# Gated cross-attention and mixture-of-experts layer on one core: scores turned by plain transposes, joint first loads, key groups 3 and 4 in two parts, a last bank in two steps, and a new order of stages

## The reference, cut

```python
def xattn(text, features):                    # text: layernorm(x) per batch
    features_n = rmsnorm(features, fn_w)
    Q = rmsnorm(text @ Wq.T + Wq_b, qn_w)
    K = rmsnorm(features_n @ Wk.T + Wk_b, kn_w)
    scores = (Q @ K.T) / sqrt(1024)            # 512 x 64 per batch
    return softmax(scores) @ features_n
def ffn(x):
    base = x @ W_base.T + b_base
    gate = softmax(x @ W_gate.T); thr = sigmoid(x @ W_thr + b_thr) / 8
    w = relu(gate - thr); w = w / sum(w)       # 8 experts, rank 16
    return base + 2 * ((x @ A.T) * w) @ B
x = x + tanh(g_xattn) * xattn(layernorm(x), ctx)
x = x + tanh(g_ffn) * ffn(layernorm(x))
```

## Time and profile before

| what | value |
|---|---|
| median of 3 runs | 478.19 us |
| the profiled execution | 478.68 us |
| its span in the trace | 476.7 us |
| around the span | 1.98 us |
| PE busy | 471.1 us, 99% |
| DVE, ACT, POOL busy | 353.9, 172.4, 121.1 us |

### The profile page before, as it was taken

One profiled execution on the slowest core, in us unless ns is written; L12 is line 12 of the kernel. 1 busy time (PEld: TensorE's weight loads), 2 busy tenths in 40 slices (PEclk: granted clock), 3 DMA queues, 4 the chain that ended last, 5 costly groups with the idle time before them and its releaser, 6 DMA issues.

```text
span 476.7 us, 6939 instructions
## 1 busy us (share of the span) xinstructions
PE 471.1 (99%) x2482; PEld 401.3 (84%) x2482; DVE 353.9 (74%) x735; ACT 172.4 (36%) x347; POOL 121.1 (25%) x110
## 2 busy tenths in 40 slices
PE   8999999999999999999999999999999999999997
PEld 6888999998887888888898888888888887888885
DVE  1379896597888967869978888868677678877732
ACT  3795541341214304217326625332241521414300
POOL 1021511003353343345242406031220402305000
PEclk9999999999999999999999999999999999999999
DMA  8995219948676369466579640221405013050202
GB/s 267 411 411 197 84 58 409 382 167 294 196 240 242 134 237 289 187 244 237 183 267 420 280 141 35 78 100 46 133 0 178 0 63 114 1 177 1 89 1 88
DMA packets 22545, 84.39 MB, mean 177 GB/s; under 512 B 2672, under 2 KB 4720, under 8 KB 19696
## 3 DMA queue, kind: packets, MB, share of 16 engines
q1 hardware_dynamic: 22368, 83.94, 48.0%
q10 hardware_dynamic: 144, 0.02, 0.0%
HBM read 61.93 MB, written 22.02 MB: 176 GB/s over the span
## 4 chain that ended last, share of the span: by engine, by line
PE 91%; DMA 6%; DVE 1%; issue 1%; SPq 1%; POOL 0%; DVEq 0%
PE bank L637 11%; PE bank L758 11%; PE bank L762 10%; PE bank L760 10%; PE bank L673 6%; PE bank L675 6%; PE bank L674 6%; PE bank L736 4%; PE bank L516 3%; PE bank L601 2%; DMA out_dram<-xs 2%; DMA xz<-xt_dram 2%; PE bank L659 2%; PE bank L658 2%; PE bank L660 2%; PE bank L738 2%
## 5 line engine op out<-in xcount | busy, mean ns | idle before, releaser
L1532 POOL TENSOR_TENSOR small<-small,tiny 128x1 f32<-128x1 f32 (+2 forms) x25 | 22.7, 907 | 163.1 <-DVE small L1165 138.4
L1506 DVE SCALAR_TENSOR_TENSOR xs<-bank,tiny,xs 128x512 f32<-128x512 f32 x60 | 43.2, 748 | 21.0 <-PE bank L762 15.0
L673 PE MATMUL bank<-xth,gram 128*128 128x512 f32 x144 | 57.3, 398 | 0.0
L675 PE MATMUL bank<-xtl,gram 128*128 128x512 f32 x144 | 56.3, 391 | 0.0
L674 PE MATMUL bank<-xth,gram 128*128 128x512 f32 x144 | 56.1, 390 | 0.0
L1560 POOL TENSOR_TENSOR sq_sum<-sq_sum,sq 128x512 f32<-128x512 f32 x24 | 32.0, 1335 | 59.0 <-DVE sq L1340 59.0
L758 PE MATMUL bank<-wh_B,zh 128*128 128x512 f32 x116 | 47.0, 405 | 0.0
L758 PE MATMUL bank<-wh_T,zh 128*128 128x512 f32 x112 | 45.9, 410 | 0.0
L762 PE MATMUL bank<-wh_B,zl 128*128 128x512 f32 x116 | 45.6, 393 | 0.0
L760 PE MATMUL bank<-wl_B,zh 128*128 128x512 f32 x116 | 45.4, 391 | 0.0
L762 PE MATMUL bank<-wh_T,zl 128*128 128x512 f32 x112 | 44.1, 393 | 0.0
(11 more groups left out here) (200 smaller groups left out, 1117.8 us busy)
## 6 DMA issues: line engine op xcount, KB each, us to landing
xst<-x_dram SPq DMA_DIRECT2D x16, 512.0 KB, 4.3
xz<-xt_dram SPq DMA_DIRECT2D x16, 512.0 KB, 7.7
out_dram<-xs SPq DMA_DIRECT2D x14, 512.0 KB, 3.7
xa<-x_dram SPq DMA_DIRECT2D x12, 512.0 KB, 3.3
x<-xa SPq DMA_DIRECT2D x12, 512.0 KB, 2.8
xs<-x SPq DMA_DIRECT2D x12, 512.0 KB, 3.9
wq_raw<-wq_dram SPq DMA_DIRECT2D x8, 512.0 KB, 14.7
t_raw_T<-wb_dram SPq DMA_DIRECT2D x4, 1024.0 KB, 16.6
```

Of the source, the lines that this page charges most:

```text
L673: pe.matmul(acc[:, :], gram[:, g, 0, :], xth[b % 2][:, r, :], start=r == ROWS[j][0], stop=False)
L675: done = pe.matmul(acc[:, :], gram[:, g, 0, :], xtl[b % 2][:, r, :], start=False, stop=r == ROWS[j][-1])
L1506: dve.scalar_tensor_tensor(out=xs[slot][:, half(h)], in0=bank[C_BANK[n_bank]][:, :], scalar=tg[:, 1:2], in1=xs[slot][:, half(h)], op0=ALU. ...
```

## The change

Six edits. (1) Context and the first two key weights come in one array `front` and one load per chunk; the weights of group 2 are only issued once the first chunk has landed. (2) `RAW_KEYS` goes from 5 to 3: groups 3 and 4 use split operands; "ct_high" stands ahead of "k01", ("split", "CT", 0) behind group 2. The squares of the context move from ACT to DVE. (3) "tops": four transposes of `st_sb` (128 columns each) in place of the four matmuls with `ident2`; ACT copies one half out of the bank, DVE adds the other, and the maxima and exponentials read `pexp` in SBUF. (4) In the last pair "fin" 0 to 2 stand ahead of product P4, P4 and the last "fin" are made in two halves of 256 columns in two banks, and each half is evicted and stored alone, the second by ACT's queue. (5) `IDLE` 4 for 5. (6) The order of stages: ("x_stat", 0), "stat" 3, ("mr", 0), "rsb" with the first "k_out" and "load_hd" move.

```diff
-    RAW_KEYS = 5
+    RAW_KEYS = 3
...
-        IDLE = 5
+        IDLE = 4
...
+        def spans(p, n):
+            if (p, n) == (NP - 1, 3):
+                return [(C_BANK["D"], 0, HALF // 2), (H_BANKS[0], HALF // 2, HALF)]
+            return [(C_BANK[whole(p)[n][0]], 0, HALF)]
...
-                         ("gates", 0), ("split", "B12", 1), ("stat", 3)]
-                extra = {0: [("weights", 3), ("chosen", 0), ("hd", 0, 1), ("gates", 1), ("shares", 3), ("split", "B22", 0), ("fn_norm", 3),
+                         ("gates", 0), ("split", "B12", 1)]
+                extra = {0: [("weights", 3), ("chosen", 0), ("stat", 3), ("hd", 0, 1), ("gates", 1), ("shares", 3), ("split", "B22", 0), ("fn_norm", 3),
...
+                if (p, name) == (NP - 1, "P4"):
+                    last += [("fin", p, n) for n in range(3)]
                 last.append(("prod", p, i))
...
-                        if c % CK == 0:
-                            pe.wait_ge(ld_wk01[c // CK], 16)
                         pe.wait_ge((a_ct, v_ct)[c % 2], c // 2 + 1)
...
-                    acc = ring_open(("weights", b), "act")
+                    acc = ring_open(("weights", b), "dve")
                     pe.wait_ge(a_st, b + 1)
-                    for j in range(TPB):
-                        done = pe.matmul(acc[:, j * S:(j + 1) * S], st_sb[:, j * P:(j + 1) * P], ident2[:, :],
-                                         start=True, stop=True)
-                    done.then_inc(p_ring, 1)
+                    transposes(acc, st_sb[:, :].rearrange("p (j t) -> p j t", j=TPB))
...
-                load_ct(c)
-                sp.dma_start(wk01[:, :, kc, :], wk[0:2].rearrange("f p c m -> p f c m")[:, :, kc, :]).then_inc(ld_wk01[c], 16)
+                sp.dma_start(ct_wk01[:, :, c, :], front[:, c, :, :]).then_inc(ld_ct[c], 16)
+            sp.wait_ge(ld_ct[0], 16)
...
-                elif stage == "ctx_norm":
-                    for c in range(2):
-                        act.wait_ge(ld_ctx[c], 16)
-                        act.activation(ctx_sq[c][:, :], ctx_raw[c][:, :], ACT.Square,
-                                       accum_out=ctx_ss[:, c:c + 1]).then_inc(a_ctx, 1)
...
+                elif stage == "tops":
+                    b, = i
+                    n = ring.number["weights", b]
+                    act.wait_ge(p_ring, ring.full(("weights", b)))
                     if b > 0:
                         act.wait_ge(v_px, b)
...
+                    act.activation(pexp[:, :, :], bank[T_BANKS[n % 2]][:, :].rearrange("p (j h s) -> p j h s", j=TPB, h=2)[:, :, 0, :],
+                                   ACT.Copy).then_inc(a_top, 1)
...
+                    dve.wait_ge(a_top, b + 1)
+                    dve.tensor_tensor(pexp[:, :, :], acc[:, :, 1, :], pexp[:, :, :], ALU.add).then_inc(ring_sem["dve"], 1)
+                    dve.wait_ge(ring_sem["dve"], ring.empty(n)[1])
+                    dve.tensor_reduce(s_top, pexp[:, :, :], AX_X, ALU.max).then_inc(v_top, 1)
```

More of the change, by code:

```diff
@@ L389, in build @@
                 first.append(("y", b, j))
+                if (b, j) == (B - 1, 4):
+                    first.append(("load_hd",))
                 if b == 0:
@@ L458, in build @@
                 last += extra.get(i, []) + ahead.get(i, [])
-            for i in range(4):
+            for i in range(3 * (p == NP - 1), 4):
                 last.append(("fin", p, i))
@@ L756, in tensor @@
                     z = z_slot[p, tok]
-                    for k in range(KH):
-                        pe.matmul(acc[:, :], zh[z][:, k, :], wh[op][:, k, :], start=opens and k == 0, stop=False,
-                                  skip_group_check=True)
-                        pe.matmul(acc[:, :], zh[z][:, k, :], wl[op][:, k, :], start=False, stop=False,
-                                  skip_group_check=True)
-                        done = pe.matmul(acc[:, :], zl[z][:, k, :], wh[op][:, k, :], start=False, stop=k == KH - 1,
-                                         skip_group_check=True)
+                    parts = [(C_BANK[n_bank], 0, HALF)]
+                    if (p, name) == (NP - 1, "P4"):
+                        parts = spans(p, 3)
+                        pe.wait_ge(v_hg, NT - 1)
+                    for part, lo, hi in parts:
+                        acc, cols = bank[part][:, 0:hi - lo], slice(lo, hi)
+                        for k in range(KH):
+                            pe.matmul(acc, zh[z][:, k, :], wh[op][:, k, cols], start=opens and k == 0, stop=False,
+                                      skip_group_check=True)
+                            pe.matmul(acc, zh[z][:, k, :], wl[op][:, k, cols], start=False, stop=False,
+                                      skip_group_check=True)
+                            done = pe.matmul(acc, zl[z][:, k, :], wh[op][:, k, cols], start=False, stop=k == KH - 1,
+                                             skip_group_check=True)
                     done.then_inc(p_prod, 1)
@@ L930, in sync @@
                     t, slot = 2 * p + j, slot_of(p, j)
+                    _, lo, hi = spans(p, n)[0]
+                    cols = slice(h * HALF + lo, h * HALF + hi)
                     sp.wait_ge(v_ev, ev_no[p, n_bank])
-                    sp.dma_start(out[t * P:(t + 1) * P, half(h)], xs[slot][:, half(h)]).then_inc(st_out[slot], 16)
+                    sp.dma_start(out[t * P:(t + 1) * P, cols], xs[slot][:, cols]).then_inc(st_out[slot], 16)
             for slot in range(4):
-                loads = sum(slot_of(p, j) == slot for p in range(NP - 1) for j in range(2))
-                sp.wait_ge(st_out[slot], 16 * (loads + 2 * (slot in (slot_of(NP - 1, 0), slot_of(NP - 1, 1)))))
+                stores = sum(slot_of(p, j) == slot for p in range(NP - 1) for j in range(2))
+                stores += sum(len(spans(NP - 1, n)) for n, (_, j, _) in enumerate(whole(NP - 1)) if slot_of(NP - 1, j) == slot)
+                sp.wait_ge(st_out[slot], 16 * stores)
         def scalar(act):
@@ L1146, in scalar @@
                                    accum_out=sg[:, 1:2]).then_inc(a_ex, 1)
+                elif stage == "fin" and len(spans(*i)) > 1:
+                    p, n = i
+                    n_bank, j, h = whole(p)[n]
+                    t, slot = 2 * p + j, slot_of(p, j)
+                    _, lo, hi = spans(p, n)[1]
+                    cols = slice(h * HALF + lo, h * HALF + hi)
+                    act.wait_ge(v_ev, ev_no[p, n_bank] + 1)
+                    act.dma_start(out[t * P:(t + 1) * P, cols], xs[slot][:, cols]).then_inc(st_out[slot], 16)
         def vector(dve):
@@ L1505, in vector @@
                         dve.wait_ge(g_x1, seq[2 * p + j] + 1)
-                    dve.scalar_tensor_tensor(out=xs[slot][:, half(h)], in0=bank[C_BANK[n_bank]][:, :],
-                                             scalar=tg[:, 1:2], in1=xs[slot][:, half(h)], op0=ALU.mult,
-                                             op1=ALU.add).then_inc(v_ev, 1)
+                    for c, (n_bank, lo, hi) in enumerate([(C_BANK[n_bank], 0, HALF)] if stage == "part" else spans(p, key)):
+                        if c > 0:
+                            dve.wait_ge(p_fin, 4 * p + key + 1 + c)
+                        cols = slice(h * HALF + lo, h * HALF + hi)
+                        dve.scalar_tensor_tensor(out=xs[slot][:, cols], in0=bank[n_bank][:, 0:hi - lo],
+                                                 scalar=tg[:, 1:2], in1=xs[slot][:, cols], op0=ALU.mult,
+                                                 op1=ALU.add).then_inc(v_ev, 1)
                 elif stage == "weights":
```

99 lines of the change are left out of this document (45 added, 54 removed), and 2 rows, old and new, of the table first.

## The result

The changed kernel takes a median of 476.49 us (20 executions, 474.56 to 479.05), the kernel before 478.25 (20 executions, 477.39 to 479.64): ratio 0.9966, 95% interval 0.9956 to 0.9976. The forecast was 474.7, range 473.5 to 476.6, a ratio of 0.9927. So it is faster, by half of what was forecast: 1.8 us are missing. Yet the execution that was profiled took 474.56, and its trace follows the forecast closely. Such a gap between one trace and a median is the subject of what follows; it shows already in the spread, 4.5 us against 2.3 before.

The account below looks back on a forecast made before the run. PE was taken to bound the kernel, busy 471.1 of 476.7 us. Front and keys 1.7, scores 1.4 and end 0.4 sum to 3.5 us: profiled execution 475.2, median 474.7 us, range 473.5 to 476.6.

Parts of the forecast that it names:

- Front, 0.7: Start of the kernel: joint loads of the first chunks cut PE's waits and gain 0.7 us.
- Rival (a): First loads: joint loads bring nothing, as bytes per us bind, not issues; 475.3 us, chance 0.17.
- rival (f): Pause before "k01": PE returns at the lower clock, losing 3.4 us; 478.1 us, chance 0.03.
- Keys, 1.16 less 0.16: Key groups 3 and 4: split operands save 1.16 us of PE, less 0.16 charged for small waits.
- Rival (c): Waits among Wq, `ctl` and the first key outputs take a full us more than 0.16; 475.7 us, chance 0.1.
- the lead of 1.59 us: Row 6 of M: DVE's release comes 1.59 us before PE needs it, capping PE's gain unless the stores start earlier.
- rival (e): Load of tile 2 of x: taking 12.8 us, it delays the stores and PE at row 6; 483.6 us, chance 0.03.
- Scores, 1.4: Score maxima in four batches: transposes save 0 + 0.41 + 0.55 + 0.44, 1.4 us in sum, bounds 1.0 and 2.0.
- the lead at `px`: Before `px`: batch 1 is ready 0.54 us before PE turns it, so some 0.4 stays; batch 0 waits 0.2 and gains nothing.
- Rival (b): Scores: the saving goes whole, with DVE the busier neighbour and the chain 0.8 us longer; 476.1 us, chance 0.09.
- The end, 0.36: Last pair: halved P4 and "fin" cost 0.11 us, shorter eviction wins 0.27, smaller store 0.2; together 0.36, bounds 0 and 0.8.

Follow-up runs that it names:

- px_rsb: Changed kernel with "shares" ahead of z in batches 1 and 2, and "rsb" and the first key outputs ahead of block 4 of Wq: 475.34 us, 0.9928.
- px_tops_old: Changed kernel with "shares" ahead of z in batches 1 and 2, and score maxima by float32 matmuls as before: 476.92 us, 0.9961.
- px_rsb_end_old: Changed kernel with "shares" ahead of z, "rsb" ahead of block 4 of Wq, and the last pair in one step as before: 475.13 us, 0.9922.
- px_front_old: Changed kernel with "shares" ahead of z in batches 1 and 2, and two loads per first chunk again: 476.35 us, 0.9943.
- px_rsb_small: Changed kernel with "shares" ahead of z, "rsb" ahead of block 4 of Wq, and two small DVE instructions moved to POOL: 474.22 us, 0.9901.

## Why the forecast was wrong, point by point

- **Front, 0.7.** Right in its mechanism. Group 2 starts at 12.1 to 12.9 in 14 of the 16 traces with joint loads (13.3 in two), 13.1 in both of before (the 13.27 of the forecast is the end of the row ahead of it, so the waits for chunks were 0.6 us and not 0.75). In none of the 16 does PE wait for a later chunk; undone, it costs 1.1 us. Rival (a) falls. What scatters the start of group 2 is the clock:
- **The clock, rival (f).** It did not happen in the profiled execution: behind a pause of 0.9 us the 32 matmuls of "k01" take 7.01 us, 0.219 each, their step at the 2.4 GHz level. The Trainium skill, "TensorE: Matmul & The Clock Gate", Part 1 on the HAM clock gate, lets the clock stand through a pause of this length; the trace agrees. But in 7 of the 16 traces with joint loads the first one to five matmuls of "k01" still go in steps of up to 0.43 (0.59 for 0.32 behind the very first), the 1.2 GHz level, and the stage takes 7.06 to 7.94 us: up to 0.9 us lost, by other means than the forecast's. The clock does not fall in the pause, it has not risen before it: all eight warm-up matmuls went in steps of 0.43 (the first 0.59). `px_rsb`, and `px_tops_old`, which has the same warm-up and loses nothing (3 and 4 matmuls of "k01"):

```profile
1.19 3.78 PE L543 MATMUL bank<-idle 128*128 128x256 f32 x8 [1.19 <-DVE idle L1186]
5.41 1.65 PE L597 MATMUL bank<-ct_wk 128*128 128x256 f32 x3 [0.43 <-ACT ct_wk L969]
```

```profile
1.19 3.78 PE L544 MATMUL bank<-idle 128*128 128x256 f32 x8 [1.19 <-DVE idle L1185]
5.49 1.13 PE L598 MATMUL bank<-ct_wk 128*128 128x256 f32 x4 [0.52 <-ACT ct_wk L973]
```

  The pages of the profile show full clock there all the same, since the record of the granted clock begins only 4.1 to 7.3 us into the span. In both traces of before the step was down to 0.22 within the ten warm-up matmuls. Whether `IDLE = 4` causes the loss or chance spared two traces is not known; the changed kernel was not run with `IDLE = 5`.
- **Keys, 1.16 less 0.16.** 0.34 to 1.14 arrive. The place of the loss was named ("rsb" on ACT behind block 4 of Wq), its size was not: 0 to 0.9 us, the more the earlier PE is, as the chain behind block 4 hangs on a load and not on PE. Rival (c) is real, at block 5 and not, as I had it, at group 4.
- **M.** In the profiled execution the lead of 1.59 us was right, and so was the load of tile 2 (DVE takes it up at 68.25; rival (e) falls). PE comes 1.74 ahead to M and keeps 1.66; with 2.2 it keeps the same 1.66. But this lead too was read off one execution: with 1.49 in front `px_rsb_end_old` keeps 0.9.
- **Scores, 1.4.** Batch 0 counted, against my step: the load that DVE had at 147.48 and that I took for fixed is issued earlier with PE (137.60 for 139.29), and DVE takes it up at 144.75 without a wait. So the wait at `px` of batch 0 did not grow to 0.6 to 0.8 us, it went. Measured, the four are worth 1.67, 0.42 each and not 0.55: the 0.99 us for an old one was its share of the chain, by the ends of rows, where the step to the next stage is 0.84 in the kernel before:

```profile
136.90 1.00 PE L702 MATMUL bank<-ident,st_sb 128*128 128x64 f32 x8
137.74 0.60 PE L547 MATMUL bank<-ident,ms 128*128 128x128 f32 x4
```

- **The failed step** is the lead at `px`. I read 0.54 us before `px` of batch 1 and 0.2 of wait in batch 0 off one execution, and took them as the kernel's. `px` stands behind a load whose issue and landing vary by 2 us each. What the old PE met seldom (undone, 0.2 us in before) costs the quicker PE 0.6 to 1.2 us of the median. How often its executions meet it is not seen, as none of its slow ones was traced. Rival (b) comes near to the measured time (476.1), but not by its cause: with the trap in place undoing the scores still costs 1.1 us, and moving the load's wait off `px` alone brought back what was lost.
- **The end, 0.36.** The second failed step, by a cost that the sum did not have: with 746 instructions of DVE a piece of code is loaded into the last store, 0.8 to 1.0 us that no row of before showed. So the last pair takes 0.62 us more than before; without that load it takes 0.27 less, near the 0.36.

With both traps out, "rsb" early and two instructions on POOL, the change is worth 4.4 us (0.9901, five executions). The forecast sum was 3.5. The missing 1.8 us are two waits on DMA, 0.6 to 1.2 of the median at `px` and 0.9 in every traced execution at the end, and in some executions up to 0.9 by the clock; against them stand 0.7 that the scores gave more and 0.75 at the sixth pair, which the sum did not have. That the profiled execution fits the forecast was luck: it meets neither the wait at `px` nor the low clock in "k01", pays the tail (0.9), and wins 0.7 more than I gave to the scores (2.13 us from M's end to the first product) and the 0.75.

Still open: why single executions of `px_front_old`, `px_tops_old` and others lie a further 2 to 5 us above their median (the one such trace, `px_front_old` at 480.81, shows 1.1 us at an eviction of x1 and 0.9 at `pt` of batch 1 as the longest waits); and whether it is DVE's number of instructions or its waits too that place the last load, since they were never changed apart (`px_rsb_small` also gives POOL two more).

## What to carry to other kernels

A lead read from one trace is one draw: where a hand-over stands in an engine's row behind a wait for a load, ask how much that load varies, and price the hand-over at its slow end. When the bound engine gets faster, move such hand-overs ahead of the load first; it cost one line here and gave a third to two thirds of what was missing. Undo a part and look at the traces as well as at the medians: the keys looked worthless largely because undoing them also shortened the code of another engine. And look at the steps of the first matmuls: a granted clock printed as full where no record of it exists says nothing.

## What the runs showed of the hardware

An instruction load takes part in the traffic of the data: one packet of q14, 0.01 MB, inside the last store, holds single packets of the store back by 0.4 to 0.9 us, and the tail is 3.3 to 3.55 us instead of 2.46 to 2.63. It goes with the length of DVE's instruction stream: moving two small instructions of 746 to another engine took 0.9 us off the tail (3.42 in `px_rsb` to 2.49). The Trainium skill, "Runtime: NRT & Kernel Launch", section Instruction fetch mechanics, says that an engine fetches its code in blocks through a DMA queue of its own and that this cost is mostly hidden; here it shows at the end, and elsewhere it was not looked for.

The time from a load's issue to its use varied by 2 us at the same place of the program (5.5 to 7.5 us), and that of a store to the load that waits for it by 2.4 us (2.7 and 5.1).

PE's clock can still stand at the 1.2 GHz level behind eight warm-up matmul records of 256 columns: steps of 0.43 us for the first one to five matmuls behind the pause in seven of 16 traces, 0.22 in the others. The rise comes at no fixed place of the program.
